# The down product of a mixture-of-experts layer as three fp32r products of split operands, and one pair of fold weights loaded later

## The reference, cut to what matters

```
scores = einsum('btd,ed->bte', x, Wg);  top 2, softmax, w
for e in range(8):
    h = silu(x @ W1[e].T) * (x @ W2[e].T)          # 352 wide
    y = y + w[..., e:e+1] * (h @ W3[e].T)          # 512 wide
```

## Time and profile before

| | us |
|---|---|
| median of 3 timed runs (lowest, highest) | 925.7 (925.33, 927.23) |
| the profiled execution | 918.66 |
| its span, first to last instruction | 917.0 |
| PE / DVE / ACT / POOL busy | 760.3 / 539.2 / 422.2 / 241.7 |
| mean granted clock of TensorE | 0.914 |

### The profile page before, as it was taken

The page is one execution under the profiler, slowest core; times in us unless marked ns, Lnnn a source line. Parts: engine busy times, 40 slices in busy tenths (PEclk is TensorE's granted clock), DMA queues, the critical chain, the costliest instruction groups (busy, mean ns, idle before and its releaser), DMA issues.

```text
span 917.0 us, 14413 instructions
## 1 busy us (share of the span) xinstructions
PE 760.3 (83%) x4708; PEld 607.0 (66%) x4708; DVE 539.2 (59%) x1136; ACT 422.2 (46%) x805; POOL 241.7 (26%) x299
## 2 busy tenths in 40 slices
PE   0899997739999999759899898898869999686774
PEld 0688775737777778758787787786627777454552
DVE  4635764446666662567646636547455667578872
ACT  2523442135555552126646637647543544444432
POOL 1200000022222202522725607507202222134431
PEclk9897998559999999659999999999999999889887
DMA  8100003944655647820100100100165442000000
GB/s 263 55 1 2 1 1 122 405 152 150 221 172 172 184 151 238 238 80 1 37 32 22 44 23 32 44 24 24 53 268 169 143 142 84 28 1 19 18 18 18
DMA packets 28623, 88.27 MB, mean 96 GB/s; under 512 B 6004, under 2 KB 9276, under 8 KB 26272
## 3 DMA queue, kind: packets, MB, share of 16 engines
q1 hardware_dynamic: 23104, 70.49, 22.2%
q0 software_dynamic: 5472, 17.18, 6.6%
HBM read 72.57 MB, written 15.07 MB: 96 GB/s over the span
## 4 chain that ended last, share of the span: by engine, by line
PE 45%; issue 23%; DVE 10%; POOL 8%; DMA 6%; ACT 5%; SPq 1%; ACTq 1%; POOLq 0%; DVEq 0%
PE PS L146 9%; PE PS L148 8%; PE PS L147 8%; POOL wraw L646 5%; PE PS L1063 3%; PE PS L1122 2%; PE PS L1432 2%; PE PS L1415 2%; ACT w_hi L738 2%; DMA raw<-wkv_in 1%; PE PS L1107 1%; PE PS L1165 1%; DMA fq_raw<-foldq_in 1%; DMA xn_scratch<-XN 1%; SPq L461 1%
## 5 line engine op out<-in xcount | busy, mean ns | idle before, releaser
L646 POOL TENSOR_TENSOR wraw<-wraw,rinv 128x361 f32<-128x361 f32 (+1 forms) x104 | 80.7, 787 | 139.1 <-DVE rinv L1623 139.1
L1466 DVE TENSOR_TENSOR w_lo<-w,w_hi 128x1408 fp32r<-128x1408 f32 x40 | 64.9, 1622 | 37.4 <-ACT w_hi L738 37.4
L834 ACT ACTIVATE wraw<-PS,nmx 128x361 f32<-128x361 f32 (+1 forms) x104 | 58.7, 565 | 38.3 <-DVE nmx L1630 30.5
L1630 DVE TENSOR_REDUCE nmx<-PS 128x1 f32<-128x361 f32 (+1 forms) x104 | 54.9, 530 | 33.7 <-PE PS L148 33.7
L738 ACT CAST w_hi<-w 128x1408 fp32r x40 | 54.7, 1370 | 20.6 <-DMA xn_scratch<-XN 10.4
L146 PE MATMUL PS<-w_hi,xt_hi 128*128 128x352 f32 x160 | 56.9, 356 | 6.5 <-DVE xt_lo L1460 6.5
L598 POOL DMA_INDIRECT xb<-xn_scratch,rows x20 | 33.0, 1649 | 108.0 <-PE PS L1037 104.9
L1633 DVE TENSOR_TENSOR pt_lo<-PS,pt_hi 128x384 fp32r<-128x384 f32 x96 | 52.2, 546 | 12.0 <-ACT pt_hi L840 11.1
L1221 PE MATMUL PS<-ident,wraw 128*128 128x128 f32 x312 | 52.1, 277 | 6.3 <-POOL wraw L646 3.7
L1063 PE MATMUL PS<-w,ht 128*128 128x512 f32 (+1 forms) x120 | 54.9, 593 | 0.6 <-DVE ht L1478 0.6
L146 PE MATMUL PS<-pf_hi,cx_hi 128*100 128x512 f32 x128 | 51.5, 402 | 3.9 <-DVE pf_lo L1776 3.9
(11 more groups left out here) (266 smaller groups left out, 2087.2 us busy)
## 6 DMA issues: line engine op xcount, KB each, us to landing
w<-w_in SPq DMA_DIRECT2D x20, 768.0 KB, 5.1
w<-w_in SPq DMA_DIRECT2D x8, 1408.0 KB, 16.1
fq_raw<-foldq_in SPq DMA_DIRECT2D x6, 1088.0 KB, 7.2
cx_raw<-ctx_scratch SPq DMA_DIRECT2D x8, 800.0 KB, 5.2
ctx_scratch<-ctxo SPq DMA_DIRECT2D x24, 256.0 KB, 2.0
wraw<-wup_in POOLq DMA_DIRECT2D x22, 256.0 KB
ys_scratch<-yb SPq DMA_DIRECT2D x20, 256.0 KB
wraw<-wdown_in POOLq DMA_DIRECT2D x4, 704.0 KB
```

Of the source, the lines that this page charges most:

```text
L646: pool.tensor_tensor(P1[slot][0:rows, 0:NK], P1[slot][0:rows, 0:NK], rinv[0:rows, jj, t:t + 1].broadcast_to((rows, NK)), ALU.mult).then_in ...
L834: act.activation(P1[t % 8][r, 0:NK], PS[r, t % 4, 0:NK], ACT.Exp, bias=nmx[r, jj, t:t + 1], accum_out=rsum[r, jj, t:t + 1]).then_inc(C["ex ...
L1466: dve.tensor_tensor(WL[which][:, :], w12_of(dve_wlo.e, which), WH[which][:, :].bitcast(F32), ALU.subtract) \
L1630: dve.tensor_reduce(nmx[r, jj, t:t + 1], PS[r, t % 4, 0:NK], AX.X, ALU.max, negate=True).then_inc(C["max"], 1)
```

## The change

`HT` becomes fp32r and is written by ACT (cast from PSUM); DVE writes the remainder `HTL`. The raw down weights of a block are cast by ACT to `W3H` (one buffer), and DVE writes their remainder `W3L` over the raw weights. `pe_y` calls `mm3`. `W3H` and `HTL` lie where the second half of `wraw` was, which held fold pair 1. So pairs 0 and 1 take the early places (start, block 6), pairs 2 to 4 come after the last up product, and pairs 5 to 7 at the last point, pair 5 into `wraw`. Three semaphores are shared with later phases, whose counts move up.

```
-            for i in range(2):
+            for i in range(1):
                 sp.dma_start(FQR[i], foldq_d[i]).then_inc(C["fq0"], 16)
...
-            for k in range(3, 6):
+            for k in range(2, 5):
                 sp.dma_start(FQR[k][:, :, :], foldq_d[k]).then_inc(C["fq1"], 16)
             store_block(NBLK - 2)
             store_block(NBLK - 1)
             sp.wait_ge(C["fq1"], 48)
             sp.wait_ge(YGS[0], 16 * TOPK)
-            for k in range(6, NP1):
+            sp.wait_ge(E["yps"], NBLK)
+            for k in range(5, NP1):
                 sp.dma_start(FQR[k][:, :, :], foldq_d[k]).then_inc(C["fq1"], 16)
...
+        def act_w3(act, i):
+            act.wait_ge(W3S[i % 2], 16 * (i // 2 + 1))
+            wait(act, E["yps"], i)
+            act.copy(W3H, W3R[i % 2][:, :]).then_inc(W3HS, 1)
+
+        def act_ht(act, i):
+            wait(act, E["htp"], i + 1)
+            wait(act, E["yps"], i - 1)
+            act.copy(HT[i % 2][:, :], PS[:, 3, 0:FHP]).then_inc(HTHS, 1)
...
                 act_silu1(act, i)
+                if i > 0:
+                    act_ht(act, i - 1)
                 if i + 1 < NBLK:
                     act_whi(act, i + 1, 0)
                     act_xt(act, i + 1)
                     act_whi(act, i + 1, 1)
                 if i > 0:
                     act_y(act, i - 1)
+                act_w3(act, i)
+            act_ht(act, NBLK - 1)
             act_y(act, NBLK - 1)
...
             pe.wait_ge(E["ht"], i + 1)
-            pe.wait_ge(W3S[i % 2], 16 * (i // 2 + 1))
+            pe.wait_ge(W3LS, i + 1)
...
+                last = mm3(pe, PS[:, 4 + i % 2, :], HT[i % 2][0:n, h], HTL[0:n, h], W3H[0:n, w], W3L[i % 2][0:n, w],
+                           c == 0, c == len(FC) - 1)
...
         def dve_ht(dve, i):
-            wait(dve, E["htp"], i + 1)
-            wait(dve, E["yps"], i - 1)
-            dve.tensor_copy(HT[i % 2][:, :], PS[:, 3, 0:FHP]).then_inc(E["ht"], 1)
+            dve.wait_ge(HTHS, i + 1)
+            wait(dve, E["yps"], i)
+            dve.tensor_tensor(HTL, PS[:, 3, 0:FHP], HT[i % 2][:, :].bitcast(F32), ALU.subtract).then_inc(E["ht"], 1)
+
+        def dve_w3(dve, i):
+            dve.wait_ge(W3HS, i + 1)
+            dve.tensor_tensor(W3L[i % 2][:, :], W3R[i % 2][:, :], W3H.bitcast(F32), ALU.subtract).then_inc(W3LS, 1)
...
                 if i > 0:
+                    dve_w3(dve, i - 1)
                     dve_ht(dve, i - 1)
```

More of the change, by code:

```diff
@@ L222, in build_kernel @@
         HB = [at(f"hb{i}", [128, FHP], MOE_AT + 20 * D + 4 * FHP * (2 + i)) for i in range(2)]
-        HT = [at(f"ht{i}", [128, FHP], MOE_AT + 20 * D + 4 * FHP * (4 + i)) for i in range(2)]
+        HT = [at(f"ht{i}", [128, FHP], MOE_AT + 20 * D + 4 * FHP * (4 + i), F32R) for i in range(2)]
         ROUTE_AT = MOE_AT + 12 * D
@@ L289, in build_kernel @@
         P1 = [wraw[:, i * 384:(i + 1) * 384] for i in range(8)]
-        FQR = [wraw[:, i * 2 * FQ:(i + 1) * 2 * FQ].rearrange("p (h n) -> p h n", h=2) for i in range(2)] + FQS
+        FQW = [wraw[:, i * 2 * FQ:(i + 1) * 2 * FQ].rearrange("p (h n) -> p h n", h=2) for i in range(2)]
+        FQR = FQW[0:1] + FQS[0:4] + FQW[1:2] + FQS[4:6]
+        W3H = at("w3_hi", [128, W3], 8 * FQ - 4 * (W12 + W3), F32R)[:, :]
+        HTL = at("ht_lo", [128, FHP], 8 * FQ + 4 * W3 - 4 * (W12 + W3), F32R)[:, :]
+        W3L = [at(f"w3_lo{i}", [128, W3], W3_AT + 4 * W3 * i, F32R) for i in range(2)]
         pd = ExitStack()
@@ L350, in build_kernel @@
         LD0 = [16 * TOPK * len(range(i, B, 3)) for i in range(3)]
+        W3HS, W3LS, HTHS = F["mag"], C["krl"], C["krh"]
         XS, W3S = [E["xs0"], E["xs1"]], [E["w30"], E["w31"]]
@@ L476, in _ @@
                 if i == 6:
-                    sp.dma_start(FQR[2][:, :, :], foldq_d[2]).then_inc(C["fq0"], 16)
+                    sp.dma_start(FQR[1][:, :, :], foldq_d[1]).then_inc(C["fq0"], 16)
                 if i == 4:
@@ L1059, in pe_y @@
             pe.wait_ge(E["ht"], i + 1)
-            pe.wait_ge(W3S[i % 2], 16 * (i // 2 + 1))
+            pe.wait_ge(W3LS, i + 1)
             wait(pe, E["yb"], i - 1)
-            for c, rows in enumerate(FC):
-                last = pe.matmul(PS[:, 4 + i % 2, :], HT[i % 2][0:rows, c * 128:(c + 1) * 128],
-                                 W3R[i % 2][0:rows, c * D:(c + 1) * D], start=(c == 0), stop=(c == len(FC) - 1))
+            for c, n in enumerate(FC):
+                h, w = slice(c * 128, (c + 1) * 128), slice(c * D, (c + 1) * D)
+                last = mm3(pe, PS[:, 4 + i % 2, :], HT[i % 2][0:n, h], HTL[0:n, h], W3H[0:n, w], W3L[i % 2][0:n, w],
+                           c == 0, c == len(FC) - 1)
             last.then_inc(E["yps"], 1)
@@ L1143, in pe_fold_m @@
         def pe_fold_m(pe, i, j):
-            if i < 3:
-                pe.wait_ge(C["fq0"], 48)
-            elif i < 6:
+            if i < 2:
+                pe.wait_ge(C["fq0"], 32)
+            elif i < 5:
                 pe.wait_ge(C["fq1"], 48)
             else:
-                pe.wait_ge(C["fq1"], 80)
+                pe.wait_ge(C["fq1"], 96)
             wait(pe, C["msb"], i - 1)
@@ L1347, in _ @@
             pe.wait_ge(C["nfl"], NP1)
-            pe.wait_ge(C["krl"], 1)
+            pe.wait_ge(W3LS, NBLK + 1)
             for k in range(12):
@@ L1729, in _ @@
                     dve_wlo(dve, i + 1, 1)
+            dve_w3(dve, NBLK - 1)
             dve_ht(dve, NBLK - 1)
@@ L1732, in _ @@
             dve_fold(dve, 1, 1)
-            dve.wait_ge(C["krh"], 1)
+            dve.wait_ge(HTHS, NBLK + 1)
             dve.tensor_tensor(WKL[:, :, :], kr_raw[:, :, :], WKH[:, :, :].bitcast(F32), ALU.subtract).then_inc(C["krl"], 1)
@@ L1844, in dve_xq @@
                 r = rstd[:, m:m + 1] if isinstance(m, int) else rstd[:, bass.ds(m, 1)]
-                wait(dve, F["mag"], m - 1)
+                wait(dve, F["mag"], NBLK + m - 1)
                 dve.tensor_scalar(xn[:, j, :], xs, mean, r, ALU.subtract, ALU.mult).then_inc(F["xn"], 1)
@@ L1854, in dve_xsub @@
             def dve_xsub(m, j):
-                wait(dve, F["mag"], m + 1)
+                wait(dve, F["mag"], NBLK + m + 1)
                 wait(dve, F["xt"], m - 1)
```

## The result

Timed on the same chip in turns, the changed kernel takes 930.74 us (median of 22 runs) and the kernel before 921.41 (22 runs): ratio 1.0096, 95% interval 1.0074 to 1.0117, so 7 to 11 us slower. The forecast was slower by 16 us, 942 us, range 933 to 954. 4.3 us of the miss is the base: the first three runs of the kernel before had a median of 925.7, all 22 have 921.41. On that base the same sum gives 937.5 and a range of 929 to 950, which holds the time. The rest is in the sum (+16.1 against +9.3), and the two profiled executions show where: 918.66 before, 929.63 after (span 928.0), +11.0; this pair lies 1.6 further apart than the medians.

What follows compares the result with a forecast made beforehand. The block loop was taken as bound by the turn through ACT, DVE and TensorE, with the down product beside it. Loop +3.2, loop end +2.3, third load +4.4, extra folds +6.2 gave +16.1 on 925.7: 942 us, range 933 to 954.

Steps and rivals of the forecast that it cites:

- the turn of a block: Block loop through ACT, DVE and TensorE: 7.56 us with a quick register load, 8.27 with a slow one, 7.70 taken.
- the cast of h: High part of transposed h, cast on ACT between silu and register load: adds 0.47 us a turn, bounds 0 and 0.48.
- one slow load in five: ACT's register load between silu and weight cast: four quick (279 ns) for one slow (989 ns), giving 7.70 us a turn.
- The reason that I gave for quick loads: Register loads starting further behind ACT's copy of `yb`, now 3.2 us, avoid the traffic of SyncE's loads and stores.
- the signs that I had named: Profile marks of a right forecast, among them silu to silu 7.5 to 7.8 us and three fold pairs at 0.50 clock.
- The end of the loop: Block 19's down product waits for its casts and ends 2.3 us later, delaying store, gathers and SyncE's next loads.
- The third load: One more 1088 KB fold load in front of the last wait: +4.4 us, between 2.7 and 5.0.
- One more pair at 1.2 GHz: One more first and second fold on TensorE behind the last wait: +6.2 us, 3.4 at full clock.
- (a): Rival, block loop: ACT's register loads stay slow, loop +13.5 us, whole +26, 952 us; chance 0.16.
- (c): Rival, block loop: TensorE's 6.7 us a block sets the time, the faster side, down to 922 us; chance 0.04.
- (b): Rival, cheap tail: folds at full clock or third load at 420 GB/s, 929 to 937 us; chance 0.13.
- (d): Rival, loop: TensorE's clock falls from idling, some 5 us per block hit, 952 to 967 us; chance 0.09.

Runs made afterwards that it cites:

- experiment 9: Changed kernel with ACT's register load moved in front of silu; ratio to the kernel before 1.0061 (1.0038 to 1.0083).
- experiment 2: Changed kernel with fold pair 5 issued right behind the last block's store, not behind the first gathered rows; ratio to the kernel before 0.9981 (0.9953 to 1.0010).
- experiment 3: Kernel before with one idle 100x384 cast more on ACT per block, between silu and the register load; ratio 0.9995 (0.9973 to 1.0016).
- experiment 8: Kernel before with ACT's register load moved in front of silu; ratio 0.9927 (0.9897 to 0.9958).
- experiment 6: Changed kernel with one idle 100x384 cast more on ACT behind the cast of h; ratio to the kernel before 1.0117 (1.0075 to 1.0158).
- experiment 7: Changed kernel with one down product in place of three, all casts and waits kept; ratio to the kernel before 1.0152 (1.0119 to 1.0185).
- experiment 1: Kernel before with only the fold part of the change (two pairs early, three at the last point), fp32 down product; ratio 1.0097 (1.0063 to 1.0131).
- experiment 4: Changed kernel without SyncE's wait for the first gathered rows before the last fold loads; ratio to the kernel before 0.9974 (0.9951 to 0.9998).
- experiment 5: Kernel before without SyncE's wait for the first gathered rows before the last two fold loads; ratio 0.9950 (0.9927 to 0.9974).

## Why the prediction was wrong, point by point

**The step that failed is the turn of a block**, a term of the right kind and the wrong size, in two places. I took 0.47 us for the cast of h in a turn with a quick load; it is 0.33 (7.09 to 7.42, and the weight cast 0.97 us behind silu in place of 0.64), mostly because neighbours on ACT overlap by 0.11 (experiment 9) and I had allowed "0.1 at most" but not subtracted it. And I took one slow load in five; in the 18 turns there was none. Together 7.42 for 7.70, in 18 turns 5.0 us: the loop came out at -1.8 for +3.2, outside even my bounds (+0.7 to +13.5). The reason that I gave for quick loads, that they would start further behind ACT's copy of `yb`, is not refuted: in the changed kernel they start 3.0 us behind it (257.86 to 260.86) and are all quick (in experiment 2 one of them took 582 ns). In experiment 3, at 1.9 to 2.7, both kinds occur. In experiments 8 and 9 they start with the copy of `yb`, just as SyncE issues its load and store, and all 19 are quick. But the two rows from which I took the rule were thin ground: in the kernel before, a load at 2.35 us took 937 ns and one at 2.38 took 307. And the load matters less than I thought, since a slow one hides under whatever ACT has to do behind silu. What the traffic has to do with it was not tried by itself.

**What bounds the loop** was read rightly: the turn through `xt_lo`, with the down product beside it (experiments 6, 7, 9). Of the signs that I had named, the cast of h behind silu, the wait for `xt_lo`, product 19 starting 3 us later against the last up product (2.8), 13 us idle in front of pair 5 (13.42) and three pairs at 0.50 all came; the turn alone, at 7.42, missed its 7.5 to 7.8. Casts of the down weights on ACT and DVE were covered, as forecast: ACT 0.66 us idle in front of each silu (forecast 0.6), w3 cast 1.49 (1.48), remainder 1.76 (1.75).

**The end of the loop.** Product 19 was to end 2.3 us later and to shift everything. It starts 4.0 us after TensorE's last transposes, its clock falls on the way (rows 351.31 and on stand 0.43 apart in place of 0.23), and it ends 10.0 us behind the issue of the middle loads in place of 6.2. But the last loads come 19.8 us behind the middle ones, before 19.1; in experiments 1 and 7, with product 19 done at 6.2 and at 5.8, it is 19.3 in both. So 3.7 us later cost 0.8 at most, and my "nothing covers it" was wrong. GpSimd's first gather, after and before, shows what hid it:

```profile
358.86 1.01 POOL L618 DMA_INDIRECT yg<-ys_scratch,slots  x1 [14.04 <-DMA ys_scratch<-yb]
```
```profile
361.16 1.01 POOL L612 DMA_INDIRECT yg<-ys_scratch,slots  x1 [13.20 <-DMA ys_scratch<-yb]
```

It comes 14.5 and 13.7 us behind the middle fold loads. In the kernel before the last store was issued 7.0 us behind these loads, while the queue that they share was still full (342 GB/s until 359 us), and the gather followed 6.7 us later; in the changed kernel it was issued 10.8 us behind them, as the last of them was landing (175 GB/s from 354 to 356 us), and the gather followed 3.7 us later.

**The third load** was put at 4.4 (bounds 2.7 and 5.0) and cost 7.0. What I missed is the traffic beside it: while SyncE's loads go, the gathers go too. 1.48 + 3.71 MB against 0.80 + 2.36 is 2.03 MB more, at 296 GB/s 6.9 us.

**One more pair at 1.2 GHz** was put at 6.2; the stretch behind the wait grew from 15.6 to 21.6, 6.0.

The tail's sum was 2.3 + 4.4 + 6.2 = 12.9 by forecast and 0.8 + 7.0 + 6.0 = 13.8 measured: near by luck, for two errors nearly cancel. Total in the profile: -1.3 - 1.8 + 13.8 + 0.4 behind the tail = +11.0 (the terms are rounded). Of the rivals, (a) and (c) did not come about; the full clock of (b) came only where the wait was taken away (experiments 4 and 5), and (d) showed itself in experiment 7 only. By (c)'s own terms its time would be 919 to 924 us; the 922 given there is neither end.

## What to carry to other kernels

Before work is taken off an engine, find the turn that sets a loop and ask whether the work is in it: here the lighter product was beside the turn and its cast in it, and with the register load out of the way both kernels needed 7.19 us a block. Ask what the room for new buffers pushes back: one load of 1088 KB moved behind a wait cost more (+12 us in experiment 1) than the loop gave (1.8). A register load belongs in the idle time in front of the instruction that starts the turn, and a wait that only orders traffic should be tried without: by themselves these gave 0.7% and 0.5%, and together with holding back the next phase's loads 1.75%, with no change of the arithmetic.

## What the runs showed of the hardware

- A register load on ACT lasts from 272 to over 1000 ns (1116 in experiment 1). It starts while ACT works on what stands in front of it, so this work hides it, and only the instruction behind it waits.
- Less work on TensorE can be slower: in experiment 7, busy 77% of the loop, its granted clock was 0.95 and the kernel 0.6% slower than the changed one, in whose loop (93% busy) it was 1.00.
- ACT instructions of 0.47 us stand 0.36 us apart when nothing waits between them (261.82, 262.18 and 262.54 in experiment 9).
- Loads of SyncE and gathers of GpSimd that go at the same time came to 283 to 296 GB/s together, with two fold loads as with three.
